# Tile 0's weight rounding on GpSimd alone, and two steps of the weight sums moved in tile 13

## The reference

```python
def _tlin(x, w, s):
    return jnp.einsum('bsi,oi->bso', x, w) * s
h = jax.nn.silu(_tlin(x, w1_w, w1_s)) * _tlin(x, w2_w, w2_s)      # 256 -> 1024, gated
h = jax.nn.gelu(_tlin(h, h1_w, h1_s), approximate=False)          # 1024 -> 1024
h = jax.nn.gelu(_tlin(h, h2_w, h2_s), approximate=False)          # 1024 -> 1024
return _tlin(h, w3_w, w3_s)                                       # 1024 -> 256
...
x = x + 0.5 * ffn(layernorm(x))
x = x + s4d(layernorm(x))        # long convolution by FFT, gelu, projection
x = x + 0.5 * ffn(layernorm(x))
```

## Time and profile before

| | us |
|---|---|
| median of 3 runs (1412.19 to 1413.75) | 1412.91 |
| the profiled execution, its own time | 1412.11 |
| its span in the trace | 1410.1 |
| TensorE busy (matmul) | 1400.1 |
| VectorE busy | 1022.3 |
| ScalarE busy | 539.2 |
| GpSimd busy | 53.5 |
| granted TensorE clock, mean over the span | 0.999 |

### The profile page before, as it was taken

The page is one execution under the profiler, slowest core; times in us unless marked ns, Lnnn a source line. Parts: engine busy times, 40 slices in busy tenths (PEclk is TensorE's granted clock), DMA queues, the critical chain, the costliest instruction groups (busy, mean ns, idle before and its releaser), DMA issues.

```text
span 1410.1 us, 18146 instructions
## 1 busy us (share of the span) xinstructions
PE 1400.1 (99%) x7214; PEld 1170.1 (83%) x7214; DVE 1022.3 (72%) x1810; ACT 539.2 (38%) x846; POOL 53.5 (4%) x45
## 2 busy tenths in 40 slices
PE   8999999999999999999999999999999999999999
PEld 5788888888878888788787888878878788898989
DVE  7777777675878888748878577785787798655454
ACT  6644342523425124232242232422414324554554
POOL 1000000000000000010000100001000010000000
PEclk9999999999999999999999999999999999999999
DMA  9001000012013121131210312012240224020200
GB/s 370 21 16 31 15 31 30 22 40 68 34 76 139 56 60 60 41 105 48 88 60 12 135 46 75 27 49 72 90 134 16 61 81 155 2 76 31 90 1 17
DMA packets 56552, 90.86 MB, mean 64 GB/s; under 512 B 2960, under 2 KB 46352, under 8 KB 54288
## 3 DMA queue, kind: packets, MB, share of 16 engines
q1 hardware_dynamic: 54640, 81.25, 17.1%
q10 hardware_dynamic: 1824, 8.39, 1.6%
HBM read 63.41 MB, written 24.12 MB: 62 GB/s over the span
## 4 chain that ended last, share of the span: by engine, by line
PE 95%; DVE 2%; ACT 2%; issue 1%; DMA 0%; POOL 0%; ACTq 0%; DVEq 0%
PE ps L1778 74%; PE ps L1903 7%; PE ps L1914 5%; PE ps L2002 3%; PE ps L2055 1%; PE ps L1754 1%; ACT junk L831 1%; DVE bits L1598 1%; PE ps L1997 1%; PE ps L1996 1%; PE ps L1969 1%; ACT h L842 0%; PE ps L2045 0%; PE ps L1979 0%; DVE raw L1593 0%
## 5 line engine op out<-in xcount | busy, mean ns | idle before, releaser
L615 ACT ACTIVATE act_o<-ps,scales 128x512 f32<-128x512 f32 x360 | 248.0, 689 | 759.8 <-PE ps L1778 757.4
L1778 PE MATMUL ps<-hid_a_hi,h 128*128 128x512 f32 x984 | 387.0, 393 | 0.0
L1778 PE MATMUL ps<-hid_a_lo,h 128*128 128x512 f32 x984 | 383.0, 389 | 0.0
L1778 PE MATMUL ps<-hid_b_hi,h 128*128 128x512 f32 x832 | 327.8, 394 | 2.0 <-ACT w L842 2.0
L1778 PE MATMUL ps<-hid_b_lo,h 128*128 128x512 f32 x832 | 324.8, 390 | 0.0
L1778 PEld LDWEIGHTS ps<-hid_a_hi,h 128*128 128x128 f32 x984 | 184.7, 188 | 40.5 <-issue 2.2
L1778 PEld LDWEIGHTS ps<-hid_a_lo,h 128*128 128x128 f32 x984 | 184.8, 188 | 40.2 <-issue 2.2
L1778 PE MATMUL ps<-hid_b_hi,w 128*128 128x512 f32 x480 | 187.3, 390 | 0.6 <-DVE gz L1734 0.6
L1778 PEld LDWEIGHTS ps<-hid_b_hi,h 128*128 128x128 f32 x832 | 156.8, 188 | 36.4 <-ACT w L842 2.5
L1778 PE MATMUL ps<-hid_b_lo,w 128*128 128x512 f32 x480 | 186.9, 389 | 0.0
L1778 PEld LDWEIGHTS ps<-hid_b_lo,h 128*128 128x128 f32 x832 | 156.8, 188 | 33.4 <-issue 1.2
(11 more groups left out here) (348 smaller groups left out, 1595.1 us busy)
## 6 DMA issues: line engine op xcount, KB each, us to landing
ks<-k_d SPq DMA_DIRECT2D x32, 512.0 KB, 3.8
raws<-in_weights SPq DMA_DIRECT2D x5, 1024.0 KB, 17.5
stage<-in_weights SPq DMA_DIRECT2D x4, 1024.0 KB, 10.8
xin<-in_x SPq DMA_DIRECT2D x8, 512.0 KB, 3.8
x_d<-xin SPq DMA_DIRECT2D x8, 512.0 KB, 2.8
z_d<-xin SPq DMA_DIRECT2D x8, 512.0 KB, 2.8
zb<-z_d SPq DMA_DIRECT2D x8, 512.0 KB, 5.0
wb<-x_d SPq DMA_DIRECT2D x8, 512.0 KB, 4.2
```

Of the source, the lines that this page charges most:

```text
L615: A(act_o[:, k % ACT_SLOTS], bank(source), func, scale=scale).then_inc(s_act, 1)
L1778: last = MM(o, weight[:, k, cols].bitcast(dt), part[:, k].bitcast(dt), start=(k == 0 and i == 0), stop=(k == n - 1 and i == len(act_) - 1))
```

## The change

It has two parts. In tile 0, GpSimd rounds all eleven chunks: 2 to 5 as they land, 6 to 10 as `see_bits` counts them, then 0 and 1. `round_weights`, `LATE_ROUNDINGS` and ScalarE's nine roundings go away, one semaphore `s_placed` counts all the copies, and the branch for long weights waits for all of them. In tile 13, the second half of the fourth sum (17) moves from the end of tile 12 to behind the gated layer, and `second_flag` moves from behind block 14 to behind block 13.

```diff
-LATE_ROUNDINGS = {(0, 13): 9, (0, 14): 10, (0, 17): 0, (0, 18): 1}
...
             if T == SEVEN_FROM:
-                engine.wait_ge(s_spare, (13, 20, 23, 23)[q])
+                engine.wait_ge(s_spare, (17, 20, 23, 23)[q])
...
-            for c in (3, 5):
+            for c in STAGED:
                 pool.wait_ge(s_w[c], 16)
-                G.tensor_copy(place(c), raw(c)).then_inc(s_placed_pool, 1)
+                G.tensor_copy(place(c), raw(c)).then_inc(s_placed, 1)
+            for i, c in enumerate(SEEN_BY_SCALAR):
+                pool.wait_ge(s_seen, i + 1)
+                G.tensor_copy(place(c), raw(c)).then_inc(s_placed, 1)
+            pool.wait_ge(s_low, 4)
+            pool.wait_ge(s_first_rounded, KH - EXACT_BLOCKS)
+            pool.wait_ge(s_u, at_u(0, KH - 1))
+            for c in range(2):
+                G.tensor_copy(place(c), raw(c)).then_inc(s_placed, 1)
             norms(0)
...
-                    if T == 0 and m == 2:
-                        round_weights(2)
...
                 if T == 0:
-                    round_weights(4)
                     for i in range(len(SEEN_BY_SCALAR)):
                         see_bits(i)
-                    for c in (6, 7, 8):
-                        round_weights(c)
...
-                    if (T, k) in LATE_ROUNDINGS:
-                        round_weights(LATE_ROUNDINGS[T, k])
...
             def sums_behind_update():
                 dve.wait_ge(s_pj, B)
-                for half in range(2):
-                    sum_half(16 + half, raw_4, half, A12, raw_2, ALU.subtract)
+                sum_half(16, raw_4, 0, A12, raw_2, ALU.subtract)
...
                 gated_low(T, KH - 1)
+                if T == SEVEN_FROM:
+                    sum_half(17, raw_4, 1, A12, raw_2, ALU.subtract)
...
-                    if T == SEVEN_FROM and k == KH + 6:
+                    if T == SEVEN_FROM and k == KH + 5:
                         second_flag()
...
-                if T == 1 and m == 0:
-                    pe.wait_ge(s_placed, 4 + len(SEEN_BY_SCALAR))
...
-                            pe.wait_ge(s_placed if kk in (0, 4) else s_placed_pool, kk // 4 + 1)
+                            pe.wait_ge(s_placed, kk // 2 + 1)
...
                         if T == 0:
-                            pe.wait_ge(s_placed, 2 + len(SEEN_BY_SCALAR))
+                            pe.wait_ge(s_placed, N_CHUNKS)
```

More of the change, by code:

```diff
@@ L300, in build @@
         s_ident, s_const, s_par, s_taps, s_tab = (sem(n) for n in ("s_ident", "s_const", "s_par", "s_taps", "s_tab"))
-        s_placed, s_placed_pool, s_raw_d, s_raw_h1, s_raw_h2, s_raw_w, s_scales, s_ahead = (sem(n) for n in (
-            "s_placed", "s_placed_pool", "s_raw_d", "s_raw_h1", "s_raw_h2", "s_raw_w", "s_scales", "s_ahead"))
+        s_placed, s_raw_d, s_raw, s_scales, s_ahead = (sem(n) for n in (
+            "s_placed", "s_raw_d", "s_raw", "s_scales", "s_ahead"))
         s_z0hi, s_z0lo, s_first_rounded, s_seen, s_wsum_0, s_flag_0, s_wmax_0, s_few = (sem(n) for n in (
@@ L418, in _ @@
                 sp.wait_ge(s_raw_d, 16)
+                sp.wait_ge(s_placed, N_CHUNKS)
                 sp.wait_ge(s_ahead, AHEAD)
-                def load_raw(t, at, done):
+                at = 0
+                for t in (w1, w2, h1, h2, w3):
                     flat = flat_of(t)
[L423 to L437, removed]
+                    sp.dma_start(flat.bitcast(F32), w_d[:, at:at + flat.shape[1]]).then_inc(s_raw, 16)
+                    at += flat.shape[1]
+                sp.wait_ge(s_raw, 16 * 5)
             def store_x(T):
@@ L831, in see_bits @@
                 A(junk[:, :].bitcast(BF16), raw(c).bitcast(U16)[:, 0::2], ACT.Copy, accum_out=words_of[:, 2 + i:3 + i]).then_inc(s_seen, 1)
[L833 to L840, removed]
-                    act.wait_ge(s_u, at_u(0, KH - 1))
-                A(place(c), raw(c), ACT.Copy).then_inc(s_placed, 1)
             act.wait_ge(s_one, 1)
@@ L1680, in _ @@
                     weigh_bits()
-                    dve.wait_ge(s_placed, 2)
-                    dve.wait_ge(s_placed_pool, 2)
+                    dve.wait_ge(s_placed, len(STAGED))
                     first_exponents()
@@ L1804, in layer_one @@
                     pe.wait_ge(s_first_rounded, m - EXACT_BLOCKS + 1)
-                if T == 1 and m == 0:
-                    pe.wait_ge(s_placed, 4 + len(SEEN_BY_SCALAR))
-                    if dt == F32:
-                        pe.wait_ge(s_raw_w, 32)
                 if m == 0:
@@ L2101, in feed_forward @@
                         if T == 0:
-                            pe.wait_ge(s_placed, 2 + len(SEEN_BY_SCALAR))
-                            if dt == F32:
-                                pe.wait_ge(s_raw_h2, 32)
+                            pe.wait_ge(s_placed, N_CHUNKS)
                         for k in range(2 * KH, PER_U):
@@ L2144, in _ @@
                     hidden_end(k, s_ahead)
-                pe.wait_ge(s_raw_h1, 16)
+                pe.wait_ge(s_raw, 16 * 5)
                 feed_forward(range(SEVEN_FROM), F32, from_=None)
```

## The result

| kernel | median of its runs, us | span of the profiled run | mean granted clock |
|---|---|---|---|
| before | 1412.7 (1410.6 to 1413.75, 6 runs) | 1410.1 | 0.999 |
| changed | 1418.78 (1416.97 to 1421.23, 6 runs) | 1417.1 | 0.996 |

The changed kernel takes 1.0046 times as long as the one before, with an interval of 1.0033 to 1.0059: slower by 6.1 us. Its profiled run took 1418.97.

A forecast was written before the change was run, and what follows sets the result against it. TensorE, busy 1400.1 of 1410.1 us, was taken as the bound. Tile 0 +7.2, clock 0, tile 13's update -0.6 and flag 0 gave +6.6 on the median 1412.91: 1419.5 us, range 1415.0 to 1424.0.

The forecast's parts named there:

- Price of a turn: Tile 0: when both have work queued, VectorE's next contending instruction waits for one GpSimd copy, 1.57 us each turn.
- Chunk 2's copy meets the mask: Tile 0, first verdict: the mask waits for GpSimd's copy, the verdict's sum stands at 18.06, TensorE loses about 1.5.
- The stall at the sum: Tile 0, second verdict: five VectorE instructions give way to copies (7.8), verdict ready at 49.8, TensorE stalls 5.2.
- more than I count: Rival, much slower: one-value and seven-value instructions take turns too, clock falls twice or for longer; +9 to +11, 1423; chance 0.15.
- Idle time of some 4 at the branch: Tile 0, sign in the new trace: after the stall at `sum_bits`, TensorE idles again about 4 at the branch.
- The 2.04 at block 16: Tile 0: TensorE's wait for ScalarE's rounding of chunk 10, at 60.76, goes; -2.04.
- The clock: Tile 0: one old slow stretch worth 1.5 goes, a new one costs the same; 0, bounds -1.5 and +1.5.
- Tile 13, -0.6 at the update: With the half sum moved, the residual update starts up to 1.2 earlier; the idle 0.55 and its slow restart go.
- Tile 13's flag: Branch to the seven products: the flag did not end the idle 0.66, so moving it brings 0; bound -0.66.
- The first one, that turns don't bite: Rival: copies slip between VectorE's instructions or overlap them, ScalarE waits go and nothing replaces them; -5.8, 1407.1; chance 0.08.
- The second, two turns to one for VectorE: Rival: VectorE goes first most of the time, the verdict is late by 3 turns, TensorE stalls 2.0; 1415.2; chance 0.10.
- a free mask (+3.5) and blocked reduces (+3 more): Tile 0: if the mask took no turns, the sum would be +3.5; if reduces took turns too, +3 more.

The follow-up runs named there:

- the shared kernels: Kernel before with tile 13's part and the roundings divided between GpSimd and ScalarE; with chunk 2 on GpSimd 1407.76, on ScalarE 1407.56.
- both kernels that only delayed the copies: Changed kernel with chunk 2's copy waiting for the first verdict, 1416.95; changed kernel with copies 6 to 10, 0, 1 behind the flag, 1416.69.
- The last kernel: Against the one before it: chunk 2 rounded by ScalarE behind block 2, chunks 3, 4 and 5 copied by GpSimd as they land; 1407.56, 0.9961 of before.
- the one before it: Kernel before with tile 13's part; GpSimd copies chunks 2 to 5 behind the first verdict, 9 and 10 behind the flag, ScalarE the others; 1407.76.

## Why the prediction was right, point by point

The median came out 0.7 us below the number given, with the mechanism that carried the forecast. Numbers of the changed kernel's trace are given less the 0.49 by which its transfers came late.

- **Price of a turn, 1.57.** Right: five turns cost 7.73 against 7.8 (1.5 to 1.6 each). The exponents' turn cost 1.85 - 0.29 = 1.56.
- **Chunk 2's copy meets the mask, +1.5.** Right. The mask took 2.00, the sum stood at 18.06, as forecast, and the first join came 1.53 later behind the first gate. The reduce and the one-value cast took no turn, though the next copy ran from 17.61 to 19.51. TensorE waited 1.4 to 2.1 at this sum in all kernels with chunk 2's copy beside the mask, and 0 to 0.9 in the others.
- **Order of the turns.** Right: the first join ran free, the next five contending instructions gave way one by one.
- **The stall at the sum, 5.2.** Under-sized by 0.9. The verdict was ready 0.85 later than worked out, because the instruction on seven values took a turn too (1.02 for 0.17). The prediction had put that under "more than I count". It did not add up in the end, since the copy it gave way to was the one that the exponents were expected to give way to: the cast ended at 54.66 against 54.5. From there to the work behind the branch the forecast took 1.2 to 1.3 and the trace has 0.86. So the forecast was 55.7 and the trace has 55.5, +9.0 for +9.2; two small errors cancelled.
- **Idle time of some 4 at the branch.** Wrong as a sign: it is 1.42. The work between the sum and the branch was put at 1.7, but took 3.35 (51.24 to 56.01, less 1.42), since it ran at the lower clock, and it began 0.85 later. The time is the same, because the flag is what the work behind the branch waits for either way. The prediction had said that a slow stretch of the first stall would lie under the second, but did not take it off the idle time.
- **The 2.04 at block 16.** Gone, as forecast.
- **The clock, 0.** Nearly right in sum (+2.03 for one slow stretch, -1.71 for the other: +0.3), within its bounds. It was one slow stretch over both stalls and 4 us of work, not one of its own behind the second. The term isn't a fixed price (last section), and that it came out near zero in the profiled pair owes something to chance.
- **Tile 13, -0.6 at the update.** Right: the start of block m = 1 moved up by 0.71 against block m = 0. The half sum in its new place cost nothing, since the instruction behind it still waited 1.01 for ScalarE.
- **Tile 13's flag, 0.** Wrong, by -0.46 in the changed kernel's trace and -0.49 with the flag moved alone, though only -0.14 with tile 13's part alone. The step that failed is the carrying over of 1.35 from one branch to the other, to show that a flag 1.73 ahead could not be the last to arrive. The bound given was -0.66, and the result lies inside.
- **Rivals.** The first one, that turns don't bite, gave 1407.1. Its time is what the shared kernels reach, 1407.8 and 1407.6, by keeping the copies out of the way of most of VectorE's work. The second, two turns to one for VectorE, is excluded by the timelines. Of the two other readings of the rule, a free mask (+3.5) and blocked reduces (+3 more), neither holds: the masks took turns and the reduces did not, 0.69 at 49.16 with a copy under it. That is how the Trainium skill, page "SBUF — State Buffer", section "Who interferes with whom", has it.
- **What is left.** A shift of +0.3 between tile 1 and tile 13 belongs to no wait that the trace shows. Another +0.3 lies behind TensorE's last product.

## What to carry to other kernels

A copy moved to GpSimd because its time lies idle is paid for by VectorE, one whole copy for each VectorE instruction that is queued beside it and wants the same access, so the move is free only where VectorE is waiting for something else or runs instructions that don't contend, such as the reduces here. Before such a move, list the VectorE instructions beside each copy and multiply, and look behind the new place as well: both kernels that only delayed the copies met the next piece of VectorE work. Here the gain of 4.7 and 5.4 us, of which tile 13's part has some 1.5 by its own median, was in giving GpSimd the six or five copies that met the least work on the path, not all eleven.

## What the runs showed of the hardware

**Turns.** With both queues full the engines alternated strictly, in the changed kernel and in the one with the copies behind the flag: each contending VectorE instruction took 1.5 to 1.7 more, be it 0.29 or 2.3 long by itself. The one on seven values, which reached a copy already begun, took 0.85 more. Not all instructions contend: a reduce took 0.69 under a copy, a cast of one value 0.15, a reciprocal of 128 x 256 values 1.75 with the copies behind the flag and 1.75 before, and the gates that read `ps` 0.75 with a copy beside them and without.

**Reads and writes.** Against GpSimd's writes, joins of two inputs ran at full speed (4.69 for two) and `tensor_scalar` instructions of 128 x 256 waited 1.49 and 1.57. The Trainium skill, page "SBUF — State Buffer", section "Who interferes with whom", has it so for two inputs; the runs agree.

**The clock after a stall is not a fixed price.** The same idle time of 2.0 at block 16 was followed by a slow stretch in the kernel before and in the one with only the flag moved, and by none in the one with tile 13's part alone, whose work there is the same. These are the windows behind it, of the flag's kernel and of tile 13's:

```profile
62.20:65.20 3.00, 3.00 (x9) 2.38 (x8) 2.83 (x7) 0.00 (x0) 0.00 (x0) 0.54 0.00 0
```

```profile
61.90:64.90 3.00, 3.00 (x14) 2.45 (x14) 2.56 (x7) 0.24 (x1) 0.00 (x0) 1.00 0.00 0
```

Nor does the length of the wait alone decide it. The kernel that writes zeros idled 3.18 ahead of 49.91 and kept the full clock, in this window and in the next (1.00 from 50 to 53):

```profile
47.00:50.00 3.00, 0.09 (x1) 0.10 (x1) 2.37 (x9) 0.42 (x1) 0.00 (x0) 1.00 0.00 0
```

And the same waits of 6.11 and 1.4 kept the clock low until about 60 in the changed kernel and until about 55 in the one with tile 0's part alone:

```profile
51.00:54.00 3.00, 2.49 (x7) 2.04 (x8) 2.86 (x6) 0.00 (x0) 1.99 (x2) 0.50 0.00 0
54.00:57.00 3.00, 1.60 (x6) 0.79 (x5) 2.44 (x7) 0.61 (x2) 0.00 (x0) 0.82 0.00 0
57.00:60.00 3.00, 3.00 (x15) 2.46 (x14) 2.90 (x5) 2.35 (x4) 0.00 (x0) 1.00 0.56 177
```

That is worth 1.6 to 2.1 us between traces whose waits are alike (78.59 against 76.99, 85.85 against 83.77 in the table's last column), about as much as most of the terms of this study. The last kernel, which has no such stall, ranges over 0.55 us in five runs, and the one before it, with 0.29 at block 8, over 2.7 in seven; tile 0's part alone ranges over 6.4 in six. Which of an execution's properties decides it is not shown; a difference of 2 us between two single traces of kernels with a stall should not be read as an effect of an edit.

**The end of the program varies too.** From the seven products to TensorE's last product all eleven traces take 187.67 (to 0.01). Behind it six take 3.3 to 3.7 us to the end, and five take 4.9 to 5.3: those with only the flag moved, with chunk 2's copy waiting, with zeros, with the copies behind the flag, and the last one. What differs is when the last 128 KB of the output land. These are the changed kernel and the one with chunk 2's copy waiting (size, us from issue to landing):

```profile
out_x<-xin SPq DMA_DIRECT2D x1, 128.0 KB, 1.7
out_x<-xin SPq DMA_DIRECT2D x1, 128.0 KB, 3.6
```

No edit touches the output. Whether these 1.5 us belong to a kernel or change from one execution to the next, one trace of each can't tell; single spans should be compared up to TensorE's last product.
